# A four-layer attention and expert kernel: layers 2 and 3 as one chain of slots, with expert weights streamed from memory

## What is computed

```python
x = x + _L0_xattn_ref(_layernorm(x), ctx, ...)   # cosine similarities
x = x + _L0_ffn_ref(_layernorm(x), ...)          # 8 gated experts of 336, all of them
x = x + _L1_xattn_ref(_layernorm(x), ctx, ...)   # one head
x = x + _L1_ffn_ref(_layernorm(x), ...)          # top 2 of 8 experts of 512, relu
x = x + _L2_xattn_ref(_layernorm(x), ctx, ...)   # 16 heads of 8, output projection
x = x + _L2_ffn_ref(_layernorm(x), ...)          # top 2 of 8 gated experts of 512, and shared ones
x = x + _L3_xattn_ref(_layernorm(x), ctx, ...)   # 16 heads of 8, output projection
x = x + _L3_ffn_ref(_layernorm(x), ...)          # top 2 of 8 experts of 256, relu, biases
```

## Time and profile before

| what | value |
|---|---|
| median of 3 runs | 3384.65 us (3383.18 to 3394.57) |
| the profiled execution | 3390.2 us |
| its span, first to last instruction | 3388.2 us |
| TensorE busy | 2448.5 us, 72% |
| VectorE busy | 1620.3 us, 48% |
| ScalarE busy | 1001.9 us, 30% |
| GpSimd busy | 887.2 us, 26% |
| mean granted TensorE clock | 0.820 |

### The profile page before, as it was taken

How to read it: one execution, slowest core, us unless ns; L and a number is a source line. 1 busy time by engine, 2 the same in 40 slices (tenths; PEclk the granted TensorE clock), 3 DMA queues, 4 the chain that set the end, 5 groups by cost and what they waited for, 6 DMA issues and landing times.

```text
span 3388.2 us, 40240 instructions
## 1 busy us (share of the span) xinstructions
PE 2448.5 (72%) x9792; PEld 1364.7 (40%) x9793; DVE 1620.3 (48%) x4173; ACT 1001.9 (30%) x3220; POOL 887.2 (26%) x891
## 2 busy tenths in 40 slices
PE   5888889983477678868687787866866846776462
PEld 2555555552354333433334334433433423333241
DVE  2444444442344455555445555545545545665442
ACT  2333333330112234323233342322422412332110
POOL 2555555552222311210302101031021031121313
PEclk7999999995688788888778898877977967877676
DMA  5111111301011100100100000010000010010112
GB/s 192 41 40 49 58 58 58 135 8 37 26 36 38 38 14 19 30 15 9 53 4 28 13 19 21 6 32 15 24 22 14 15 31 18 22 30 17 35 55 56
DMA packets 110910, 121.45 MB, mean 36 GB/s; under 512 B 16300, under 2 KB 83054, under 8 KB 109422
## 3 DMA queue, kind: packets, MB, share of 16 engines
q1 hardware_dynamic: 98526, 95.15, 8.5%
q0 software_dynamic: 12288, 25.19, 2.6%
HBM read 56.84 MB, written 63.44 MB: 35 GB/s over the span
## 4 chain that ended last, share of the span: by engine, by line
PE 55%; DVE 15%; issue 11%; POOL 10%; ACT 5%; DMA 1%; another core or an unknown queue 1%; DVEq 1%; SPq 0%; POOLq 0%; ACTq 0%
PE up L736 8%; PE D L651 7%; PE Y L831 7%; PE up L810 6%; PE B L632 4%; PE Y L745 3%; PE A L616 3%; POOL list L1458 3%; PE up L616 3%; PE up L820 2%; DVE xn L1019 2%; PE D L563 2%; ACT prob L906 2%; DVE nmax L1050 2%; PE up L813 2%
## 5 line engine op out<-in xcount | busy, mean ns | idle before, releaser
L1430 POOL TENSOR_TENSOR vare<-moments,eps 128x4 f32<-128x4 f32 x64 | 13.1, 205 | 1396.4 <-DVE moments L1010 1396.0
L651 PE MATMUL D<-probT,va 128*32 128x512 f32 x512 | 290.9, 662 | 60.9 <-DVE ao L1071 60.9
L563 PE MATMUL D<-const,xn 128*128 128x128 f32 x256 | 65.9, 407 | 356.8 <-DVE xn L1019 356.8
L1504 POOL TENSOR_TENSOR hid<-tg,uc 112x512 f32<-112x512 f32 x192 | 247.3, 1288 | 283.1 <-ACT uc L949 224.5
L1270 DVE SCALAR_TENSOR_TENSOR tg<-tg,up 112x512 f32<-112x512 f32 x192 | 131.7, 686 | 317.6 <-ACT tg L945 317.6
L745 PEld LDWEIGHTS Y<-wd,hid 112*128 112x128 f32 x1536 | 212.4, 202 | 124.6 <-issue 86.7
L831 PEld LDWEIGHTS Y<-wd,hid 128*128 128x128 f32 x1536 | 204.5, 206 | 143.6 <-issue 121.7
L1469 POOL DMA_INDIRECT ytmp<-list,pos_back x192 | 185.1, 964 | 292.9 <-DVE pos_back L1194 190.6
L906 ACT ACTIVATE prob<-A,nmax 128x128 f32<-128x128 f32 x512 | 181.3, 366 | 267.6 <-DVE nmax L1050 115.1
L831 PE MATMUL Y<-wd,hid 128*128 (+1 forms) x1536 | 234.5, 300 | 30.9 <-DVE x L1356 12.9
L906 ACT ACTIVATE prob<-up,nmax 128x128 f32<-128x128 f32 x512 | 181.4, 369 | 239.4 <-PE B L632 172.7
(11 more groups left out here) (174 smaller groups left out, 4375.9 us busy)
## 6 DMA issues: line engine op xcount, KB each, us to landing
list<-xn SPq DMA_DIRECT2D x21, 1536.0 KB, 9.4
uc<-list SPq DMA_DIRECT2D x240, 64.0 KB
list<-uc SPq DMA_DIRECT2D x240, 64.0 KB, 1.5
ctxT<-in_ctxT SPq DMA_DIRECT2D x32, 192.0 KB, 2.4
list<-xn,pos_now POOLq DMA_INDIRECT x192
ytmp<-list,pos_back POOLq DMA_INDIRECT x192
wg<-in_wg SPq DMA_DIRECT2D x1, 2304.0 KB, 17.5
wu<-in_wu SPq DMA_DIRECT2D x1, 2304.0 KB, 22.5
```

Source lines behind the costliest of these rows:

```text
L563: mm = pe.transpose(D[:, t * P:(t + 1) * P], rows[:, t, :], ident)
L651: mm = pe.matmul(D[r, :], va[:, t, r], probT[:, q % 2, :, :].rearrange("p i q -> p (i q)"), start=True, stop=True)
L1504: pool.tensor_tensor(hid[0:rows, i % HRING, :], tg[0:rows, i % 2, :], uc[0:rows, i % 2, :], ALU.mult).then_inc(hid_ready.sem, 1)
```

## The change

Layer 0 and the first half of layer 1 do the same work as before. What else is changed:

- **Unrolled.** All loops are written out, and every address but the expert's weights and the tile's rows is a constant.
- **Slots.** The 16 pairs (layer, group) of layers 2 and 3 make one `CHAIN`, eight slots to a pair. A slot has the scores, maxima and exponentials of two quads, and the transposes, evacuations and value products of the two quads before. Pieces of the tail of the group behind (output product, second norm, routing, scatter) and of the head of the group ahead (gather, combine, first norm, projections) stand at fixed slots r = 0 to 7, the same for each group. q, kbd, va, context, moments and other buffers are doubled, probabilities have four.
- **Tiles in slots.** The tiles are one sequence of eight segments; `SPAN` says over which slots a segment is spread, so that a slot has none to three or four turns, half of them in its middle and half near its end. The shared tiles of layer 2 are segments of their own. The last segment comes behind the slots, with the last combinations.
- **Streamed weights.** In layer 0, SyncE copies the weights of layers 1 to 3 within memory so that a row block holds all of one expert. Each routed tile then loads its expert's weights (512, 768 or 321 KB) into a ring of five.
- **Hidden rows turned from the start.** `tile_up` makes four products of 128 columns with the weights as the stationary operand in place of one of 512 columns with the rows as that, so the hidden rows come out turned. `transpose_hidden` and its evacuation are gone.
- **Sums late.** The probabilities are no longer divided. The reciprocals of the sums of a sequence are spread by one product with the identity (`spread_sums`), and `pick_heads` multiplies by them.
- **Between engines.** Both evacuations of a pair, and the spreading of the keys, are on ScalarE.

```diff
+WRING = 5
+PAIRS = QUADS // 2
+CHAIN = [(K, g) for K in (2, 3) for g in range(GROUPS)]
+SPAN = {1: (-6, 24), 2: (24, 42), 3: (42, 56), 4: (57, 74), 5: (74, 88), 6: (105, 136)}
+SLOTS = range(-9, PAIRS * len(CHAIN) + PAIRS)
...
+            for g in range(1, GROUPS):
+                step(g)
+            for S in SLOTS:
+                slot(S)
+            end()
...
+            def load_weights(n):
+                L, u, j = TILES[n]
+                r = ROUTED_NO[n]
+                e = sp.value_load(table[0:1, u % 2, 0, j:j + 1], min_val=0, max_val=EXPERTS - 1)
+                if r == 0:
+                    sp.wait_ge(relaid, 16 * 10)
+                if r >= WRING:
+                    m = max(k for k in range(n) if ROUTED_NO[k] == r - WRING)
+                    sp.wait_ge(tile_y_read if TILES[m][0] == 3 else tile_y, m + 1)
+                sp.dma_start(w_tile[:, r % WRING, 0:WIDTH[L]], wts[L][bass.ds(e * P, P), :])\
+                    .then_inc(wt_loaded[r % WRING], 16)
...
+                for c in range(HIDDEN[L] // P):
+                    mm = pe.matmul(bank_g[:, c * P:(c + 1) * P], w[:, c * P:(c + 1) * P], rows, start=True, stop=True)
+                mm.then_inc(tile_g, 1)
```

The slot of TensorE, and under it those of ScalarE and VectorE, with their waits left out:

```diff
+                if now:
+                    scores(*now, r)
+                if last:
+                    transpose_probs(*last, rl, 0)
...
+                tile_turns(first)
+                if last:
+                    transpose_probs(*last, rl, 1)
...
+                tile_turns(second)
+                if last:
+                    weigh_values(*last, rl)
...
+                if last:
+                    evacuate_probs(*last, rl, 0)
+                if now:
+                    exponentials(*now, r, 0)
+                if r == 3 and ahead:
+                    evacuate_norm(*ahead, LN1)
+                if r == 5 and ahead:
+                    spread_keys(*ahead)
+                if now:
+                    exponentials(*now, r, 1)
+                tile_turns(first)
+                if last:
+                    evacuate_probs(*last, rl, 1)
...
+                if before_last and rb % 2:
+                    pick_heads(*before_last, rb // 2)
+                if last and rl % 2:
+                    invert_sums(*last, rl // 2)
+                if r == 3 and behind:
+                    normalize(*behind, LN2)
+                if r == 6 and behind:
+                    find_rows(*behind)
+                if now:
+                    score_max(*now, r, 0)
+                    score_max(*now, r, 1)
+                if r == 5 and behind:
+                    rank_sum(*behind)
+                tile_turns(first)
+                if r == 1 and behind:
+                    add_attention(*behind)
+                if r == 2 and behind:
+                    norm_moments(*behind, LN2)
+                if r == 2 and ahead:
+                    combine(*ahead)
+                    norm_moments(*ahead, LN1)
```

More of the change, by code:

```diff
@@ L65 @@
 STEPS = GROUPS // 2
[L66 removed]
+ROUNDS = [(1, 0), (1, 4), (2, 0), (2, 4), (3, 0), (3, 4)]
 MAX_TILES = 40
[L68 to L70 removed]
 LIST = STEPS * N
@@ L389, in first_group @@
             eng.wait_ge(rest_loaded, 4 * 16)
[L391 to L415, removed]
-        def up_of(b, j):
-            return G if tile_layer(b, j)[0] == 2 or j % 2 == 0 else U
-        def pair(b, j):
-            return j if BLOCKS[b][2] == 2 else j - routed[b]
-        def run(first, trip, before_block, step, eng):
+        def turns_of(k):
+            a, b = FIRST[k], FIRST[k + 1]
+            inside = lambda n: n if a <= n < b else None
+            return [(inside(n - DEPTH), inside(n), inside(n - 1)) for n in range(a, b + DEPTH)]
@@ L859, in _ @@
-            run(lambda: first_group(pe, pre), trip, before_block, step, pe)
+                        pe.wait_ge(shared_loaded, 3 * 16)
+                    rows = x2T[:, g % 4, t * P:(t + 1) * P]
+                else:
+                    r = ROUTED_NO[n]
+                    pe.wait_ge(xsT_done, r + 1)
+                    pe.wait_ge(wt_loaded[r % WRING], 16 * (r // WRING + 1))
+                    rows = xsT[:, r % 2, :]
+                both = L == 2 or n and TILES[n - 1][0] == 2
+                if n > (not both):
+                    pe.wait_ge(tile_h, n if both else n - 1)
@@ new lines, in tile_turns @@
+            def tile_turns(turns):
+                for down, rows, up_ in turns:
+                    if down is not None:
+                        tile_down(down, ROUTED_NO[down + DEPTH if rows is not None else
+                                                  (up_ + 1 if up_ is not None else down + 1)])
+                    if rows is not None and TILES[rows][1] is not None:
+                        transpose_rows(rows)
+                    if up_ is not None:
+                        tile_up(up_)
@@ L862, in _, with end @@
+            def end():
+                tile_turns(turns_of(7))
+            run(lambda: first_group(pe, pre), trip, step, slot, end, pe)
         @block.scalar
         def _(act):
-            act.wait_ge(w_loaded[0], W_TOTAL[0])
+            act.wait_ge(w_loaded, W0_DMAS)
             for K in (1, 2, 3):
@@ L1415, in _, with end @@
+            def end():
+                turns = turns_of(7)
+                for g in range(GROUPS):
+                    tile_turns(turns[11 * g:11 * (g + 1)])
+                    recall(4, g)
+                    combine(4, g)
+            run(lambda: first_group(dve, pre), trip, step, slot, end, dve)
         @block.gpsimd
```

1122 lines of the change are left out of this document (606 added, 516 removed).

## The result

The changed kernel takes 2875.36 us (median of 4 runs, 2873.15 to 2885.76), the one before 3386.29 beside it: a ratio of 0.8494 (0.8468 to 0.852), so 15% less. The forecast was 3063 us in a range from 2885 to 3265, with 0.90 on faster. The profiled execution has a span of 2883.9 us where the sum had 3066, so 182 us have to be found.

A forecast was written before the change was run, and what follows sets the result against it. TensorE, busy 72% of the span, was taken as the busiest engine. Start 902, layer 1 208, around the attention 69, slots 1666 and end 221 summed to a 3066 us span, so 3063 us, range 2885 to 3265.

The forecast's parts named there:

- the slot chain: In a slot empty of tiles, TensorE, ScalarE and TensorE's weighing follow one another, both product pairs priced serially: 8.6 us.
- theory A: Formed after the measurement: score and value product pairs run side by side, the whole of the missing 1.7 us a slot.
- slot 3: Slot 3 of each group: VectorE's late moments, combination and normalizing make its exponentials start 4.6 us late.
- the clock: In the slots, TensorE's granted clock taken as 0.85, adding 1.25 us a slot, so 10.85.
- rival (b): In the slots, the clock sinks to 0.67: 1.5 us more in 100 slots, 3215 us in total; chance 0.09.
- Heads and tails: Head and tail work in the slots mostly fits TensorE's 2.9 us gap; two slots do not hide it, adding 7.8 a group.
- rival (e): The change does not overlap; waits keep heads and tails in line: 2080 us for the slots, 3480 total; chance 0.02.
- Rival (a): Everything overlaps, VectorE's late work is made up, clock stays full: slots 9.6, dense 16, total 2885 us; chance 0.14.
- Dense slots: In 28 slots with three layer-2 tile turns, up products wait for VectorE's passes: 18 us each.
- Tiles: On TensorE, four narrow products cost about one wide; a layer-2 tile falls from 3.16 to 2.78 us.
- SyncE and the end: Behind the slots, SyncE, never idle, sets the pace at 3.6 us a tile; with combinations and store, 221 us.
- rival (c): SyncE becomes the bound at 2.1 us a load: end +94, layer 1 +76, dense slots +30, total 3265; chance 0.07.

## Why the prediction was off

**The step that failed** is the slot chain: "two score products 1.72" and "Then TensorE weighs two quads, 1.85". At the high clock they measured 1.06 and 1.05, since the two products of each pair run side by side. The chain was right in its order and in its other terms (copy 0.60, eight exponentials 2.8, second copy 0.60 to 0.66), and an empty slot at the high clock came to 6.8 where I wrote 8.6. What I had in hand were single quads, each with its own pair of instructions on the same strip; they could only show the serial price. I took that for the bound from above and below alike. My sum should have had a low end of one product's time for two. By the runs the pairs are worth some 144 to 157 of the 193 us in the slots, up to 187 (1.46 x 128) if all of it passed through; so they are the most of it, but not the whole that theory A claimed. With the pairs kept apart, the slots measured 1690 us against my 1666. Without the waits' own price (0.71 x 0.77 x 128 = 70 us) that is 1620, so about 46 us of my slots were too long for other reasons. I can't divide those; the terms for slot 3 and for the clock, both below, are among them.

**The clock.** I took 0.85 in the slots; it was 0.81 to 0.85 in those with one or two tiles, 0.92 in the dense ones, 0.56 in the 17 without tiles, and 0.82 over all. So rival (b), the clock sinking, did happen, in one stretch. A slot of it shows the lower level, 1.2 GHz:

```profile
2259.71 1.22 PE L708 MATMUL A<-kbd,qT 32*128 32x512 f32 x1
...
2261.72 1.11 PE L716 MATMUL B<-const,prob 128*128 128x128 f32 x4
...
2266.80 1.92 PE L729 MATMUL D<-probT,va 128*32 128x512 f32 x4 [2.10 <-ACT probT L1044]
```

The transposes follow the scores after 2.01 us (1.06 at the higher level) and take 1.11 for 0.66, and the weights take 1.92 for 1.05. So TensorE's part of the chain is 2.3 us longer, where my price for a chain wholly at 1.2 GHz was 4.2. The plainest slots of this stretch are 9.0 us long; at the higher level one takes 7.18 - 0.52 = 6.7. The two whole groups of it, at 0.54 and 0.59, took 77.0 and 75.3 us. I had 76.6 without any loss to the clock, so that agreement is luck: the pairs made each slot shorter and the clock made most of them longer by about as much. My explanation of a low clock by idle gaps is not borne out by these rows alone: TensorE was busy 77% of the stretch at 0.57 and 75% of the one at 0.92, though the first percentage is itself drawn out by the low clock.

**Heads and tails.** They overlap, as forecast, and rival (e), that waits keep them in line, is dead. The longest slot of a group without tiles is the one that ends with slot 3's maximum (11.9 us against 7.5 to 9.7 in the others of its group but slot 5), and slot 5 has 10.8. The places are right. For slot 5 so is the size: its eight exponentials with the keys between them take 5.1 us for 2.8, and I had +2.4. For slot 3 it is not. Its first maximum stands 4.33 and 5.24 us behind the slot's scores in the two groups without tiles, where 2.11 is usual, so it is 2.2 and 3.1 late, and I had 4.6. In four groups with a layer-2 tile a slot it is 10.09 us behind them, against 1.70, and the slot ahead of it takes 16.5 to 17.0: there the gated passes stand in VectorE's queue ahead of the moments and the combination, and my sum had only 0.65 for the tile.

**Rival (a)** had 2885, and the time is 2875. Its number came true, but not by its mechanism. It had slots of 9.6 and 16 at a full clock because VectorE's lateness is made up. They are 9.9 and 17.2 at 0.82, and they got there because TensorE's share is smaller.

**Dense slots** took 17.2 for 18. In them the up products of a turn wait for VectorE's second pass of the turn before, as in the path I gave, where the second turn came 4.7 and the third 3.2 us behind the one before. The first two turns of one stand 3.8 apart in the timeline:

```profile
1612.38 1.06 PE L866 MATMUL up<-xsT,w_tile 128*128 128x128 f32 x8
...
1616.15 1.13 PE L866 MATMUL up<-xsT,w_tile 128*128 128x128 f32 x8 [0.82 <-DVE hid L1511]
```

**Tiles.** Narrow products cost what the earlier trace rows said. A stream of eight, behind another one in a dense slot, takes 1.06 us:

```profile
1723.03 1.06 PE L870 MATMUL up<-xsT,w_tile 128*128 128x128 f32 x8
```

With 0.27 for one alone that is (1.06 - 0.27)/7 = 0.11 us for one narrow float instruction, a quarter of a wide one's 0.43. By the rule of the Trainium skill that I weighed against the rows ("TensorE: Matmul & The Clock Gate", section "Back-to-back issue gap"), four narrow ones should have cost 2.5 times a wide one. The trace does not agree with that ratio for this data. Layer 1 came to 201 for 208.

**SyncE and the end.** I had 1.2 us an item and 3.6 a tile. Measured are 1.11 and 3.33, seen in the regular part of the last round (SyncE's timeline: weights, store, rows):

```profile
2680.61 0.34 SPq L557 DMA_DIRECT2D w_tile<-wt  x1
2681.71 0.35 SPq L564 DMA_DIRECT2D list<-uc  x1
2682.82 0.34 SPq L546 DMA_DIRECT2D uc<-list  x1
```

So SyncE sets the pace between the combinations, and it never reached the 2.1 us an item of rival (c). Yet the end took 234 for 221. The gathers that precede a combination start at 2688.66, 2733.99, 2779.05, and then at 2814.74, 2828.34, 2841.75, 2855.21 and 2868.70. Three stand between the tiles, and five behind the last one, 13.5 us apart. I had four and four, at 14. The tiles with their three combinations take 164 us (to 2813.5), for which I had 160, and the tail 70 for 56 and 5. So most of the miss is the fifth combination. In the first part my terms were off in both senses. A tile is cheaper on SyncE (133 us for 40 where I had 144), but a combination costs about 9, as eleven tiles with one take 45.3 us (2733.99 - 2688.66) and not 11 x 3.33 = 36.6, where I had 4. VectorE waits for the gathers with the next tile's result behind it, so SyncE waits too, in the view of waits of the end:

```profile
SPq L604 <- DVE x L1365: 62.9, 5, 13.2
SPq L557 <- DVE uc L1498: 23.2, 3, 7.8
```

The first row is the five combinations of the tail, the second the three between the tiles. "SyncE never idle" was wrong.

**Streamed weights** cost at most 0.6%, and perhaps nothing, as forecast, at 161 GB/s in dense slots.

**A slip in rival (c).** Its +76 for layer 1 does not follow from its 6.35 us a tile: ten tiles are then 63.5 us a step against 51, which is +50 in four steps. The top of the range would have been 26 us lower. Nothing hangs on it.

## What to carry to other kernels

Before you price two small products that stand next to each other, see which rows and columns of the array each one uses. If their strips are disjoint, the pair costs what one does, and a trace of a kernel that never issues such pairs can't show it. Give the term a low end.

When a pass is moved to an idler engine, look at what stands ahead of it in that engine's queue, in each kind of slot. Here the same move made the slots where no gated pass stood ahead of it 42 us shorter, and made the others 30 us longer when it was made everywhere.

## What the runs showed of the hardware

- Two float products on different 32-row strips, or into different 32-column strips, run at once: four instructions of 512 columns in 1.05 us, where two on one strip take 1.04. Held apart by a wait they take 2.1 to 2.2 us.
- The granted clock of TensorE stood at 0.57 over 152 us in which TensorE was busy for 117, and it was 0.92 in a stretch busy to the same share. What tells the two apart was not tried.
- In the regular part of the end SyncE issues one transfer with an offset from a table every 1.11 us.
